# A fused attention and look-up FFN kernel: the look-up steps get places of their own on ScalarE and VectorE, and ScalarE makes all eight leaves

## The chip, the cores and the metric

The kernel runs on one core of a Trainium2 chip. The metric is the device time of one execution in microseconds, the median of several runs. The kernel before takes 1107.08 us (three runs, 1107.05 to 1108.62).

A core has five engines, each with its own queue of instructions that it works off strictly in order: PE (TensorE, matrix products), ACT (ScalarE), DVE (VectorE), POOL (GpSimd) and SP (SyncE, which here issues DMAs). They wait for each other by semaphores only.

## The reference, cut to what matters

x is 2 x 2048 x 512, the four attention matrices are 512 x 512. The three FFN matrices aren't given as numbers but as indices from 0 to 15 into a table `lut` of 16 values.

```python
def attn(x, Wq, Wk, Wv, Wo):            # x is layernormed
    q, k, v = x @ Wq, x @ Wk, x @ Wv    # einsum bse,ef->bsf
    scores = einsum('bes,bfs->bef', q^T, k^T) / sqrt(16)   # 512 x 512 per batch
    return einsum('bef,bfs->bes', softmax(scores), v^T)^T @ Wo

def ffn(x, lut, gate_idx, up_idx, down_idx):   # x is layernormed
    gate, up = x @ lut[gate_idx].T, x @ lut[up_idx].T      # 1376 x 512
    return (silu(gate) * up) @ lut[down_idx].T             # 512 x 1376

x = x + attn(layernorm(x), Wq, Wk, Wv, Wo)
x = x + ffn(layernorm(x), lut, gate_idx, up_idx, down_idx)
```

## The kernel before, in words

**Stages.** The 4096 tokens are 8 blocks of 512. First comes the Gram matrix of the normalised x for both batches (stage "gram", 32 steps). From it and the weights come, all as 512 x 512 products in four items each: PROD, SCORE (with its softmax), TURN_V, MIX and FOLD, for batch 0 and 1; in the end one matrix per batch stands for the whole attention. Then each block is multiplied by it ("attend"), added, normalised again, turned ("x2") and sent through the FFN: 11 chunks of 128 inner rows, for each a gate and an up product (24 matmuls of 128 x 512) and a down product (12). The first two blocks are interleaved by hand: in `first_plan` G is a gate and up product of the first block, H of the second, D a down product of the first, T, A and X prepare the second block. From the third block on the code is regular.

**Precision.** Every operand is split in a high part (ACT writes it with a cast: `mat_y_hi`, `x2t_hi`, `h_hi`, `w_hi`) and a low part (DVE subtracts: `mat_y_lo`, `x2t_lo`, `h_lo`, `w_lo`), and each product is three matmuls. So each result of PE goes over ACT and then over DVE before PE can use it again.

**The look-up.** The FFN weights, 33 tiles of 128 x 512 (tile u is gate, up or down of chunk u // 3), are built in SBUF from the indices beside all this. Per tile u: DVE takes the high bit of the index (`find_high`, L1249) and three masks of the lower bits (`find_bit`, L1244). For each of 8 values j of the three lower bits a *leaf* is made, lut[j] + high bit * (lut[j + 8] - lut[j]). Seven of them are ACT's (`make_leaves`, L791, one ACTIVATE each), leaf 4 is DVE's own (L1275, one TENSOR_SCALAR). Seven *merges* (`merge`, L1237, COPY_PREDICATED under a mask) then pick among the leaves into `picked`, ACT casts that to `w_hi` (`weight_high`, L808) and DVE subtracts for `w_lo` (`weight_low`, L1253). There is little room: the leaves share five `part` buffers and two `picked`, so a leaf waits until a merge has read what its buffer held, and merges wait for leaves. PE's gate product of chunk c waits for `w_lo` of tile 3c, the up product for that of 3c + 1, the down product for that of 3c + 2.

**The order.** One list, `timeline`, sets the order on all engines: each engine runs over it and does its own part of each entry. In the kernel before the look-up is in that list too. A tile is ten steps (`OPS`), and an entry ("look", k) makes ACT do the leaves that `leaves_at(k)` lists and DVE the k-th step of its generator `look_up`. So both engines have their look-up work at the same places of the list. How many steps go where is by constants for the first stages (`LOOKS_GRAM`, `LOOKS_TAKE`, `looks`), and for `first_plan` by `share`, which spreads what is left evenly over the time that PE is expected to need.

## Time and profile before

| what | us |
|---|---|
| median of three runs | 1107.08 |
| the profiled execution | 1108.86 |
| its span in the trace | 1107.0 |
| PE busy in the span | 1028.1 |
| DVE busy / ACT busy | 491.6 / 467.8 |

The page gives the busy time of each engine and cuts the span in slices. "Granted clock" (PEclk) is the share of its full 2.4 GHz that PE was given; at its lower level, 1.2 GHz, it is 0.5, and slices that hold both levels lie between. The look-up is all in the first 430 us. From there to the end PE is busy without gaps worth mentioning but for one of some 10 us before the last product; what happens there isn't touched by the change. In a row of a timeline an [x <-engine tile line] at the end is the idle time before that instruction and what ended it. Durations of neighbours overlap (an instruction starts before the one ahead has wholly ended), so that the pace of an engine is read from start to start.

### The profile page before, as it was taken

To read this page: it belongs to the slowest core of one execution; us is meant where nothing else is said; L and a number is where in the kernel's file an instruction comes from. 1 tells how busy PE (TensorE), PEld (TensorE's weight loads), DVE (VectorE), ACT (ScalarE), POOL (GpSimd) and SP (SyncE) were. 2 spreads that over 40 slices of the span, in tenths; PEclk is the share of its full clock that TensorE was granted. 3 is DMA by queue.
4 is the path that set the end of the run, shared out by engine and by line. 5 is a ranking of instruction groups with operands and counts; after the bars stand their busy time and mean duration, and the time that the engine had idled before them with its cause. 6 is when DMAs were issued, how large, how long until landed. Compare 5 with 4: busy or idle time off the path is not lost.

```text
span 1107.0 us, 13011 instructions
## 1 busy us (share of the span) xinstructions
PE 1028.1 (93%) x4744; PEld 844.5 (76%) x4744; DVE 491.6 (44%) x1016; ACT 467.8 (42%) x753; POOL 137.8 (12%) x135
## 2 busy tenths in 40 slices
PE   5888986979889897999999999999999999999997
PEld 4777775767668775788888888888888888888885
DVE  5786867978878987332213122312221222212001
ACT  4987767777867884122122212211221222122110
POOL 4422000000000000002011111111111111111111
PEclk9988998989979999999999999999999999999999
DMA  8853010230101114530022000201020010000000
GB/s 280 266 198 91 8 60 6 84 119 6 46 8 65 60 51 158 207 129 1 1 76 77 1 1 1 78 1 62 15 76 1 1 41 36 1 1 38 1 1 38
DMA packets 31756, 66.04 MB, mean 60 GB/s; under 512 B 3584, under 2 KB 17168, under 8 KB 27088
## 3 DMA queue, kind: packets, MB, share of 16 engines
q1 hardware_dynamic: 26912, 63.06, 15.9%
q10 hardware_dynamic: 4752, 2.16, 0.7%
q8 instruction: 39, 0.64, 0.2%
q0 software_dynamic: 32, 0.01, 0.1%
q14 instruction: 21, 0.17, 0.0%
HBM read 44.18 MB, written 21.04 MB: 59 GB/s over the span
## 4 chain that ended last, share of the span: by engine, by line
PE 66%; DVE 12%; ACT 12%; issue 8%; POOL 1%; DMA 1%; ACTq 0%; POOLq 0%; DVEq 0%
PE bank L1050 34%; PE bank L1058 19%; PE bank L992 8%; ACT part L791 4%; DVE part L1237 3%; PE bank L1093 2%; DVE picked L1237 2%; ACT picked L791 1%; PE bank L1006 1%; PE bank L1039 1%; DVE bn L1214 1%; DVE w_lo L1253 1%; ACT idx_out L872 1%; DVE part L1275 1%; ACT xg_n L882 1%
## 5 line engine op out<-in xcount | busy, mean ns | idle before, releaser
L1050 PE MATMUL bank<-x2t_hi,w_hi 128*128 128x512 f32 (+1 forms) x704 | 278.3, 395 | 22.6 <-ACT h_gate L944 10.3
L1050 PE MATMUL bank<-x2t_hi,w_lo 128*128 128x512 f32 (+1 forms) x704 | 276.8, 393 | 0.0
L1050 PE MATMUL bank<-x2t_lo,w_hi 128*128 128x512 f32 (+1 forms) x704 | 276.6, 393 | 0.0
L1450 DVE TENSOR_TENSOR h_full<-bank,h_gate 128x512 f32<-128x512 f32 (+1 forms) x66 | 45.6, 691 | 396.6 <-PE bank L1050 396.6
L1050 PEld LDWEIGHTS bank<-x2t_hi,w_hi 128*128 128x128 f32 (+1 forms) x704 | 132.1, 188 | 55.6 <-issue 20.6
L791 ACT ACTIVATE part<-high_bit,lut,lut_step 128x512 f32<-128x512 uint8 x198 | 155.4, 809 | 27.3 <-DVE part L1237 24.9
L1050 PEld LDWEIGHTS bank<-x2t_lo,w_hi 128*128 128x128 f32 (+1 forms) x704 | 132.1, 188 | 30.3
L1050 PEld LDWEIGHTS bank<-x2t_hi,w_lo 128*128 128x128 f32 (+1 forms) x704 | 132.4, 188 | 29.5
L740 POOL TENSOR_TENSOR h_lo<-h_full,h_hi 128x512 fp32r<-128x512 f32 (+1 forms) x66 | 85.2, 1291 | 508.1 <-ACT h_hi L968 508.1
L965 ACT ACTIVATE h_gate<-bank 128x512 f32<-128x512 f32 (+1 forms) x66 | 39.4, 598 | 256.3 <-PE bank L1050 256.3
L1058 PE MATMUL bank<-w_hi,h_hi 128*128 128x512 f32 (+1 forms) x324 | 129.6, 400 | 0.1
L1058 PE MATMUL bank<-w_lo,h_hi 128*128 128x512 f32 (+1 forms) x324 | 126.6, 391 | 0.0
L1058 PE MATMUL bank<-w_hi,h_lo 128*128 128x512 f32 (+1 forms) x324 | 126.3, 390 | 0.0
L968 ACT CAST h_hi<-h_full 128x512 fp32r<-128x512 f32 (+1 forms) x66 | 41.0, 621 | 188.2 <-DVE h_full L1450 188.2
L1237 DVE COPY_PREDICATED part<-bit_mask,part 128x512 f32<-128x512 uint8 x132 | 98.2, 744 | 1.2 <-ACT part L791 1.2
L745 POOL TENSOR_TENSOR rstd<-var,power 128x4 f32<-128x4 f32 x20 | 20.9, 1047 | 429.8 <-DVE var L1227 429.8
L1237 DVE COPY_PREDICATED picked<-bit_mask,part 128x512 f32<-128x512 uint8 x99 | 70.3, 739 | 1.6 <-ACT picked L791 1.6
L1058 PEld LDWEIGHTS bank<-w_lo,h_hi 128*128 128x128 f32 (+1 forms) x324 | 60.8, 188 | 13.1
L1058 PEld LDWEIGHTS bank<-w_hi,h_hi 128*128 128x128 f32 (+1 forms) x324 | 60.9, 188 | 12.1 <-POOL h_lo L740 0.5
L1058 PEld LDWEIGHTS bank<-w_hi,h_lo 128*128 128x128 f32 (+1 forms) x324 | 61.0, 188 | 11.7
L1093 PE MATMUL bank<-xg_hi 128*128 128x256 f32 (+2 forms) x128 | 46.9, 367 | 19.6 <-DVE xg_lo L1253 16.7
L992 PE MATMUL bank<-m_hi,xt_hi 128*128 128x512 f32 x112 | 44.1, 393 | 1.0 <-DVE xt_lo L1313 1.0
(148 smaller groups left out, 1353.3 us busy)
## 6 DMA issues: line engine op xcount, KB each, us to landing
xg<-in_L_attn_x SPq DMA_DIRECT2D x8, 1024.0 KB, 6.3
out_dram<-x1a SPq DMA_DIRECT2D x5, 1024.0 KB, 3.9
x1a<-in_L_attn_x SPq DMA_DIRECT2D x4, 1024.0 KB, 4.8
x1b<-in_L_attn_x SPq DMA_DIRECT2D x3, 1024.0 KB, 4.8
m_hi<-m_scratch SPq DMA_DIRECT2D x3, 1024.0 KB, 5.1
m_lo<-m_scratch SPq DMA_DIRECT2D x3, 1024.0 KB, 7.2
out_dram<-x1b SPq DMA_DIRECT2D x3, 1024.0 KB, 3.9
idx_raw<-in_L_ffn_gate_idx SPq DMA_DIRECT2D x10, 256.0 KB, 6.2
```

The lines of the kernel that those rows point to most:

```text
L740: return pool.tensor_tensor(out_, whole, high.bitcast(F32), ALU.subtract)
L745: pool.tensor_tensor(scale[:], var[:], power[:], ALU.pow).then_inc(rstd_made, 1)
L791: act.activation(tile, high, ACT.Identity, bias=entry, scale=step).then_inc(leaf_made, 1)
L872: act.copy(dst, src).then_inc(idx_laid, 1)
L965: act.activation(h_gate[0:n, :], bank[4][0:n, :], ACT.Silu).then_inc(silu_done, 1)
L968: act.copy(h_hi[c % 2][0:n, :], h_full[0:n, :]).then_inc(h_hi_done, 1)
L992: last = pe.matmul(out_, a, b, start=(i == 0 and j == 0), stop=(i == len(terms) - 1 and j == 2))
L1050: last = pe.matmul(tile[0:n, :], a, x, start=(k == 0 and j == 0), stop=(k == K - 1 and j == 2))
L1058: last = pe.matmul(bank[t][:], a, x, start=start and j == 0, stop=stop and j == 2)
L1093: last = pe.matmul(bank[4 * batch + m][:, cols], a[:, rows_of], b[:, cols], start=start and j == 0, stop=stop and j == 2)
L1237: return dve.copy_predicated(keep[:], bit_mask[bit][:], other[:])
L1450: dve.tensor_tensor(h_full[0:n, :], bank[5][0:n, :], h_gate[0:n, :], ALU.mult).then_inc(h_done, 1)
```

## The change

The constants and the function `share` that placed ("look", k) entries are gone, and with them these entries. Two strings take their place, `ACT_LOOKS` and `DVE_LOOKS`: the k-th character says, in base 36, how many look-up steps that engine does ahead of the k-th entry of the list. ACT gets a generator `look_up` of its own, with one step for each leaf, each fetch of indices and each `w_hi`. DVE's generator yields after nearly every instruction, so that its steps are smaller. Leaf 4, DVE's until now, goes to ACT: 33 instructions leave DVE, 33 come to ACT, and the semaphore `own_leaf_made` goes. Six of the eight leaves of tile u + 1 are made ahead of `w_hi` of tile u (`LEAVES_AHEAD`); before it was five of ACT's seven. PE, POOL and SP keep their instructions in their order.

```diff
-        LEAVES = [1, 0, 3, 2, 5, 6, 7]
-        OWN_LEAF = 4
-        LEAVES_NEXT = {4: [1], 5: [0], 6: [3], 7: [2], 8: [5]}
-        LEAVES_SAME = {1: [6], 2: [7]}
+        LEAVES = [1, 0, 3, 2, 5, 4, 6, 7]
+        LEAVES_AHEAD = 6
...
+        ACT_LOOKS = (
+            "0000000000000000000000000000000000000000000000000000000000000000000000000000000000000001000000000000"
...
+        def with_looks(counts, steps):
+            for k, entry in enumerate(timeline):
+                for _ in range(int(counts[k], 36) if k < len(counts) else 0):
+                    next(steps)
+                yield entry
+            assert next(steps, None) is None
...
+            def look_up():
+
+                yield from make_leaves(0, LEAVES[:LEAVES_AHEAD])
+                for u in range(U):
+                    yield from make_leaves(u, LEAVES[LEAVES_AHEAD:])
+                    if u + 1 < U:
+                        yield from make_leaves(u + 1, LEAVES[:LEAVES_AHEAD])
+                    act.wait_ge(picked_done, u + 1)
+                    if u + 3 < U:
+                        fetch_idx(u + 3)
+                        yield
+                    weight_high(u)
+                    yield
...
-            for stage, arg in timeline:
+            for stage, arg in with_looks(ACT_LOOKS, look_up()):
...
                     merge(0, y, z).then_inc(merged, 1)
-                    tile, high, step, entry = make_leaf(dve, u, OWN_LEAF)
-                    dve.tensor_scalar(tile, high, step, entry, ALU.mult, ALU.add).then_inc(own_leaf_made, 1)
                     yield
...
-                    dve.wait_ge(leaf_made, leaf_count(u, 5))
-                    dve.wait_ge(own_leaf_made, u + 1)
+                    dve.wait_ge(leaf_made, leaf_count(u, 4))
                     merge(0, w, five).then_inc(merged, 1)
```

**First place, ACT between the softmax and the FOLD stage.** `mat_y_hi` is the high part of a MIX product; a row with `lut_step` is a leaf, `w_hi` the cast of a finished tile. Before:

```order
L912 CAST wb_hi<-bank 128x4x128 x2
L791 ACTIVATE part_164<-high_bit_166,lut,lut_step 128x512
L912 CAST mat_y_hi_111<-bank 128x512
L835 ACTIVATE xn_first<-x1a,shift_kept_188,rstd_kept_186 128x512
L791 ACTIVATE part_162<-high_bit_166,lut,lut_step 128x512
L912 CAST mat_y_hi_111<-bank 128x512
L835 ACTIVATE xn_first<-x1a,shift_kept_188,rstd_kept_186 128x512
L791 ACTIVATE part_160<-high_bit_165,lut,lut_step 128x512
L791 ACTIVATE picked_158<-high_bit_165,lut,lut_step 128x512
L912 CAST mat_y_hi_111<-bank 128x512
L835 ACTIVATE xn_first<-x1a,shift_kept_188,rstd_kept_186 128x512
L791 ACTIVATE part_162<-high_bit_165,lut,lut_step 128x512
```

And now, from the last `wb_hi` on:

```order
L879 CAST wb_hi<-bank 128x4x128 x4
L879 CAST mat_y_hi_111<-bank 128x512
L802 ACTIVATE xn_first<-x1a,shift_kept_188,rstd_kept_186 128x512
L879 CAST mat_y_hi_111<-bank 128x512
L802 ACTIVATE xn_first<-x1a,shift_kept_188,rstd_kept_186 128x512
L879 CAST mat_y_hi_111<-bank 128x512
L802 ACTIVATE xn_first<-x1a,shift_kept_188,rstd_kept_186 128x512
```

Between the last `sbias` of the softmax and the last of the four `mat_y_hi`, ACT had 11 leaves and a `w_hi`; now it has 2 leaves. Nine leaves have moved ahead of it, among the softmax items, or behind it.

**Second place, ACT at the second block's x2.** From the silu of G4 (`h_gate`) to `x2t_hi`, the turned input of the second block. Before:

```order
L944 ACTIVATE h_gate<-bank 128x512
L791 ACTIVATE picked_159<-high_bit_166,lut,lut_step 128x512
L791 ACTIVATE part_162<-high_bit_166,lut,lut_step 128x512
L791 ACTIVATE part_161<-high_bit_166,lut,lut_step 128x512
L791 ACTIVATE part_160<-high_bit_166,lut,lut_step 128x512
L958 CAST h_hi_77<-h_full 128x512
L855 CAST x2t_hi<-bank 128x512 x2
L784 DMA idx_in_170<-idx_scratch 128x512
L808 CAST w_hi_55<-picked_158 128x512
L791 ACTIVATE part_164<-high_bit_166,lut,lut_step 128x512
L791 ACTIVATE part_162<-high_bit_166,lut,lut_step 128x512
L855 CAST x2t_hi<-bank 128x512 x2
```

And now:

```order
L907 ACTIVATE h_gate<-bank 128x512
L746 ACTIVATE part_160<-high_bit_166,lut,lut_step 128x512
L746 ACTIVATE part_163<-high_bit_166,lut,lut_step 128x512
L739 DMA idx_in_171<-idx_scratch 128x512
L761 CAST w_hi_54<-picked_158 128x512
L746 ACTIVATE part_164<-high_bit_166,lut,lut_step 128x512
L921 CAST h_hi_77<-h_full 128x512
L822 CAST x2t_hi<-bank 128x512 x2
L746 ACTIVATE part_162<-high_bit_166,lut,lut_step 128x512
L746 ACTIVATE part_160<-high_bit_165,lut,lut_step 128x512
L746 ACTIVATE picked_158<-high_bit_165,lut,lut_step 128x512
L822 CAST x2t_hi<-bank 128x512 x2
```

Here the count alone doesn't change (six leaves and a `w_hi`), but ahead of this piece, from the second block's normalisation `xn_second` on, it does: up to the silu of G4 there were 10 leaves and two `w_hi`, now there are 4 leaves and none.

**Third place, DVE in the steady part of `first_plan`.** A pair (G or H) gives `h_full`, ACT casts its high part, DVE subtracts for the low one. Before:

```order
L1244 TENSOR_SCALAR bit_mask_167<-idx_in_170 128x256
L1436 TENSOR_TENSOR h_full<-bank,h_gate 128x512
L1253 TENSOR_TENSOR h_kept_lo<-h_full,h_kept_hi 128x512
L1237 COPY_PREDICATED picked_159<-bit_mask_169,part_163 128x512
L1237 COPY_PREDICATED picked_158<-bit_mask_167,part_160 128x512
L1237 COPY_PREDICATED part_161<-bit_mask_167,part_162 128x512
L1275 TENSOR_SCALAR part_163<-high_bit_165,lut_step,lut 128x512
```

And now:

```order
L1200 COPY_PREDICATED part_163<-bit_mask_167,part_164 128x512
L1397 TENSOR_TENSOR h_full<-bank,h_gate 128x512
L1216 TENSOR_TENSOR w_lo_67<-picked_159,w_hi_56 128x512
L1216 TENSOR_TENSOR h_kept_lo<-h_full,h_kept_hi 128x512
L1200 COPY_PREDICATED part_160<-bit_mask_167,part_162 128x512
```

A look-up instruction now stands between `h_full` and the low part that waits for ACT's cast of it. Of the 14 pairs after the second block's x2 that still had look-up work behind them none had that before; now all 15 have at least one.

## Rows read from the trace of the kernel before

**Rows 1.** The page: the span, and PE's busy time, share and instructions.

```profile
span 1107.0 us, 13011 instructions
PE 1028.1 (93%) x4744; PEld 844.5 (76%) x4744; DVE 491.6 (44%) x1016; ACT 467.8 (42%) x753; POOL 137.8 (12%) x135
```

**Rows 2.** Stretches: length, busy per engine (instructions), PEclk, DMA share, GB/s.

```profile
0.00:153.97 153.97, 127.16 (x729) 110.66 (x729) 110.22 (x242) 115.45 (x200) 38.10 (x55) 0.96 0.50 162
153.97:181.40 27.43, 14.91 (x65) 11.75 (x64) 22.69 (x47) 23.90 (x45) 0.00 (x0) 0.86 0.02 5
181.40:239.95 58.55, 51.34 (x224) 41.16 (x225) 46.70 (x97) 41.49 (x64) 1.39 (x1) 0.94 0.20 76
239.95:311.44 71.49, 58.85 (x249) 47.34 (x249) 57.74 (x123) 53.69 (x81) 1.01 (x1) 0.88 0.10 39
311.44:425.90 114.46, 103.74 (x432) 83.44 (x432) 96.74 (x199) 89.27 (x133) 0.00 (x0) 0.96 0.13 46
425.90:1107.00 681.10, 672.13 (x3048) 550.17 (x3048) 157.51 (x313) 144.06 (x234) 97.26 (x78) 1.00 0.11 42
```

**Rows 3.** PE's timeline: start, us, instruction, idle before and its releaser.

```profile
159.56 0.50 PE L992 MATMUL bank<-wa_hi,mat_x_hi 128*128 128x512 f32 x1 [2.54 <-DVE mat_x_lo L1407]
...
181.40 0.76 PE L992 MATMUL bank<-mat_y_hi,wb_hi 128*128 128x512 f32 x1 [9.06 <-DVE mat_y_lo L1389]
...
239.95 0.77 PE L1050 MATMUL bank<-x2t_hi,w_hi 128*128 128x512 f32 x1 [6.16 <-DVE x2t_lo L1326]
...
291.71 0.47 PE L1050 MATMUL bank<-x2t_hi,w_hi 128*128 128x512 f32 x1 [1.98 <-ACT h_gate L944]
...
305.88 1.97 PE L1039 MATMUL bank<-ident,xn_second 128*128 128x128 f32 x8 [4.86 <-DVE x2t_lo L1326]
311.44 0.77 PE L1050 MATMUL bank<-x2t_hi,w_hi 128*128 128x512 f32 x1 [3.59 <-DVE x2t_lo L1326]
...
425.90 0.48 PE L1050 MATMUL bank<-x2t_hi,w_hi 128*96 128x512 f32 x1 [1.75 <-DVE w_lo L1253]
```

**Rows 4.** DVE's timeline in the softmax: one of three alike.

```profile
148.14 0.69 DVE L1253 TENSOR_TENSOR wa_lo<-raw,wa_hi 128x512 fp32r<-128x512 f32 x1 [0.38 <-ACT wa_hi L896]
```

**Rows 5.** ACT's timeline at the end of MIX.

```profile
178.58 1.52 ACT L791 ACTIVATE part<-high_bit,lut,lut_step 128x512 f32<-128x512 uint8 x2
179.99 0.58 ACT L912 CAST mat_y_hi<-bank 128x512 fp32r<-128x512 f32 x1
```

**Rows 6.** ACT's timeline at the first block's x2.

```profile
232.33 0.80 ACT L791 ACTIVATE part<-high_bit,lut,lut_step 128x512 f32<-128x512 uint8 x1
...
238.51 2.03 ACT L855 CAST x2t_hi<-bank 128x512 fp32r<-128x512 f32 x4
```

**Rows 7.** ACT's timeline at the second block's x2.

```profile
300.60 0.57 ACT L944 ACTIVATE h_gate<-bank 128x512 f32<-128x512 f32 x1
...
304.40 1.06 ACT L855 CAST x2t_hi<-bank 128x512 fp32r<-128x512 f32 x2
```

**Rows 8.** DVE's timeline around a pair in the steady part.

```profile
404.45 0.74 DVE L1237 COPY_PREDICATED part<-bit_mask,part 128x512 f32<-128x512 uint8 x1
405.10 0.53 DVE L1275 TENSOR_SCALAR part<-high_bit,lut_step,lut 128x512 f32<-128x512 uint8 x1
405.55 0.67 DVE L1436 TENSOR_TENSOR h_full<-bank,h_gate 128x512 f32<-128x512 f32 x1
406.91 0.69 DVE L1253 TENSOR_TENSOR h_kept_lo<-h_full,h_kept_hi 128x512 fp32r<-128x512 f32 x1 [0.69 <-ACT h_kept_hi L958]
```

**Rows 9.** Groups by line, 312 to 426 us: count, busy, mean ns, idle before.

```profile
L1253 DVE TENSOR_TENSOR h_kept_lo<-h_full,h_kept_hi 128x512 fp32r<-128x512 f32 x9 | 6.2, 692 | 8.0 <-ACT h_kept_hi L958 8.0
L1253 DVE TENSOR_TENSOR h_lo<-h_full,h_hi 128x512 fp32r<-128x512 f32 x5 | 3.5, 692 | 4.3 <-ACT h_hi L958 4.3
...
L791 ACT ACTIVATE part<-high_bit,lut,lut_step 128x512 f32<-128x512 uint8 x78 | 60.5, 807 | 8.8 <-DVE part L1237 8.7
L808 ACT CAST w_hi<-picked 128x512 fp32r<-128x512 f32 x13 | 8.0, 617 | 7.6 <-DVE picked L1237 6.7 <-issue 0.8
```

More of the change, by code:

```diff
@@ L305, in preln_attention_ghost_ffn @@
         timeline = []
-        looked = [0]
-        def look(n, limit):
-            for _ in range(min(n, OPS * limit - looked[0])):
-                timeline.append(("look", looked[0]))
-                looked[0] += 1
-                if looked[0] % OPS == 0:
-                    timeline.append(("built", looked[0] // OPS - 1))
         def settle(g):
@@ L323, in stats, with normalised @@
             timeline.append(("stats_shift", g))
-        def normalised(n, limit):
-            timeline.append(("norm", n))
-            look(1 if n < K * (number[(SCORE, 0)] + 1) else 2, limit)
-            timeline.append(("norm_low", n))
-        def room(n):
-            return 12 if n < K * (number[(MIX, 0)] + 1) else 15 if n < K * (number[(FOLD, 0)] + 1) else 21
+        def normalised(n):
+            timeline.extend([("norm", n), ("norm_low", n)])
         idx_per_tile = [(0, 1, 2, 2)[i % 4] if i < T * GB else (i >= T * GB + 4) + (i == T * NG - 1) for i in range(T * NG)]
@@ L1355, in _ @@
             first = one_block[0]
-            looks = look_up()
-            for stage, arg in timeline:
+            for stage, arg in with_looks(DVE_LOOKS, look_up()):
                 if stage == "lut_step":
```

104 lines of the change are left out of this document (36 added, 68 removed).

## The prediction, written before the changed kernel ran

> **What bounds the kernel now.** I read the page first. PE is busy for 1028.1 of 1107.0 us [rows 1], so the other engines matter only where PE waits for them. The stretches show where that is [rows 2]: behind 425.90 PE idles 9 us in 681, in front of it 70 us in 426 (153.97 - 127.16 = 26.8, then 12.5, 7.2, 12.6 and 10.7), with a granted clock under 1. Nothing behind 425.90 is touched, so whatever the change is worth is the time at which PE gets there.
>
> Then PE's own timeline for the gaps and what ended them [rows 3]. None of the large ones between 150 and 312 us is ended by the look-up itself. They end with `mat_x_lo`, `mat_y_lo`, `x2t_lo` or `h_gate`, results of ordinary products on their way over ACT and DVE. The reader is to see in ACT's rows why these were late: a row with `lut` stands right in front of the awaited cast [rows 5, 6]. The look-up is in the way there, not wanted there. Only in the last stretch it is the limit itself: the up product of chunk 10 waits for `w_lo` at 425.90 [rows 3]. There DVE is busy 96.7 of 114.5 us and ACT 89.3 [rows 2], and of DVE's idle 17.7 us, 12.3 go into 14 waits for ACT's cast of h [rows 9].
>
> **The change part by part.** The sum is made against the profiled execution: span 1107.0, time 1108.9, which is 1.8 over the median of 1107.08.
>
> *Softmax to MIX.* In the first batch's softmax a leaf stands between ACT's scaling and its cast `wa_hi`, and DVE idles 0.38 for it, three times [rows 4]; the new order puts the leaves behind the cast. The chain is later than PE already (PE waits 2.54 for it at 159.56 [rows 3]), so about 1 us comes back. Two leaves per item instead of one fit in DVE's and ACT's waits for each other. Bounds: 2.5 won (the gap gone), 2 lost (two leaves more than the waits hold, at 0.7 each, with a w_hi). I take -1.
>
> *MIX to FOLD, the largest gap.* PE stopped at 181.40 - 9.06 = 172.34. All it needs is one cast and one subtraction: 0.58 for `mat_y_hi` [rows 5], 0.69 as for DVE's other subtractions of this shape [rows 4], and some 0.2 between the engines: 1.5 us. In truth two leaves stand in front of the last cast [rows 5], and DVE had merges between too. The new order has no leaf among the four casts. 9.06 - 1.5 = 7.5 us won. Bounds: 7.5, and 4 if `xn_first`, which stays between, and late work from the softmax hold it up. I take -7.5.
>
> *First block's x2.* Its normalised rows are done when the leaf at 232.33 starts, and `x2t_hi` starts at 238.51: 6.2 us [rows 6]. Between them stood six leaves and two casts; now two leaves and the same two casts. From start to start a leaf takes 1.41 / 2 = 0.70 us [rows 5]. Four leaves less are 2.8 us, and one wait for a merge between them goes (0.7): -3.5 of the 6.16 [rows 3]. Bounds 2.5 and 4.7.
>
> *Second block's x2.* Three PE gaps belong together: 1.98, 4.86 and 3.59, sum 10.4 [rows 3]. ACT had 10 leaves and two w_hi between the normalisation and the silu of G4, now 4 leaves: 6 x 0.70 + 2 x 0.5 = 5.2 us earlier. The silu at 300.60 and `x2t_hi` at 304.40 [rows 7] come that much earlier, which covers the 4.86 and leaves about 2.4 of the three gaps. -8. Bounds 5 and 9.5.
>
> *The last stretch.* 311.44 to 425.90, 114.5 us. What was left out above has to be done here: of the merges, 106 instead of 96 remain behind the second x2, of the leaves 118 instead of 91. DVE: its 96.7 us of work [rows 2] grow by 10 merges at 0.65 (405.10 - 404.45 [rows 8]), masks and one pair (3.0), and shrink by 13 leaves of its own at 0.45 (405.55 - 405.10 [rows 8]): 96.7 + 6.5 + 3.0 - 5.9 = 100.3. The 0.69 behind each `h_full` [rows 8], 12.3 in all [rows 9], is filled by the look-up step that now stands there. ACT: 27 leaves more at 0.70, two w_hi and a pair more: 89.3 + 19 + 2.5 = 110.8 to the last tile, about 103 to tile 31, the one that the up product at 425.90 needs. PE's own work is 103.7, or 99 at the full clock. So three engines need 97 to 104 us where now 114.5 pass. Nothing says that the waits of ACT for merges vanish (8.7 and 6.7 [rows 9]); I leave 5 us for waits: 108, which is -6.5. Bounds: -11 with none, and the rivals below on the other side.
>
> The Trainium skill speaks against this part: "ScalarE: Activation LUTs", section "Rules for kernel authors", says that additions and multiplications belong on VectorE, not on ScalarE. The trace agrees on the price of one: the same leaf takes 0.45 us on DVE and 0.70 on ACT, by starts. By the rule the 33 leaves moved would cost 33 x 0.25 = 8 us of engine time; the rival "paid back with interest" below is what that would look like.
>
> *The clock.* PE got 0.86, 0.94, 0.88 and 0.96 in the four stretches behind 153.97 [rows 2]: 3.8 + 3.5 + 8.6 + 4.6 = 20 us of full-speed work not granted, part of it in the gaps. After the 9.06, 6.16 and 3.59 us gaps PE's first matmul lasts 0.76 to 0.77, after the 1.98 and 1.75 ones 0.47 to 0.48 [rows 3]: with short gaps the 2.4 GHz level stays. Between 0 and 9 us come back; I take -3.
>
> *The gram stage and new waits.* In 0 to 153.97 ACT is busiest of the three (115.4 with 110.2 for DVE [rows 2]); leaf work starts with smaller bites there and catches up by 70 us: -1 (bounds +2 and -3). Against all this +4 for waits that show only when the order changes, since ACT gets 33 x 0.70 = 23 us more work by 430 us. Bounds 0 and 10.
>
> Sum: -1 - 7.5 - 3.5 - 8 - 6.5 - 3 - 1 + 4 = -26.5. From the median: 1107.1 - 26.5 = 1080.6; I say **1081**.
>
> **The rivals.**
>
> *Paid back at the old pace.* The merges not yet done at the second x2 are 10 more, 1.4 tiles. Before, 96 merges (13.7 tiles) took 114.5 us there: 8.36 us a tile. If that pace is not one of busy engines but of the ring (leaf waits for merge, merge for leaf, w_hi for picked, five buffers), it stays: 106 / 7 = 15.1 tiles x 8.36 = 126.5, +12 in the last stretch. The stages ahead still bring -1 - 7.5 - 3.5 - 8 - 1 = -21. Sum -9: **1098**. For it: ACT waits for merges and `picked` for 15 us there [rows 9]. Against it: 12.3 of DVE's 17.7 idle us are at `h_lo` [rows 9] and not at merges, so that DVE's work and those waits set the pace.
>
> *Paid back with interest: slower.* One mechanism: ACT becomes the bound of the last stretch. Each tile takes the old pace and the eighth leaf on top, 8.36 + 0.70 = 9.06 us; 15.1 x 9.06 = 137, +22.5. The stages ahead bring -21, the clock nothing, and the waits of +4 stand: +5.5, **1112**. It is slower than before once a tile takes more than (114.5 + 17) / 15.1 = 8.7 us. For it: ACT's 110.8 us of work is more than PE's. Against it: ACT had 25 us idle there (114.5 - 89.3), and the 12.3 us that DVE waited at `h_lo` are filled whatever ACT does.
>
> *All waits gone.* The last stretch at 104, the clock with its 7 us, no new waits: 1107 - 1 - 7.5 - 4.5 - 9.5 - 10.5 - 7 = **1067**.
>
> *Nothing.* Another chain, hidden now, is just behind each gap and the gaps only change names: within 0.2%, 1107.
>
> **How the numbers follow.** My case 63% (1068 to 1092), old pace 19% (1092 to 1105), with interest 8%, all waits gone 7%, nothing 3%. 0.2%, or 2.2 us, is about what a measurement of this kernel tells from no change. Faster by more: 63 + 19 + 7 = 89%; within: 3%; slower: 8%. The range for 8 in 10 leaves out the outer parts of the last stretch's cases: **1068 to 1102**.
>
> **What the changed profile would show.** MIX to FOLD: a PE gap near 1.5 us, the clock still up behind it. x2t_lo of the first block: 2.7 us instead of 6.2. Second block: the three gaps together under 3. DVE in the last stretch: hardly any idle at `h_lo`, no line with own leaves, busy over 92%. ACT over 95% busy there, with leaves of 0.70 from start to start. PE's gaps there still end with `w_lo` or `h_gate`, some 5 to 8 us in sum. PE's part behind the look-up's end stays at its 681 us. I am wrong if the second x2 isn't some 20 us earlier than 311.44, or if the stretch from there to the up product of chunk 10 takes over 115 us.

## The result, and the profile after

The changed kernel takes **1059.28 us** (median of 4 runs, 1057.82 to 1060.47). The kernel before takes 1107.85 in the same series (4 runs). The ratio is 0.9561 with a 95% interval of 0.9544 to 0.9577. The forecast was 1081, range 1068 to 1102: the sign is right, and the gain is 48.6 us where 26 were forecast. The profiled execution has a span of 1058.6 us. In a few of the series below one or two executions took far longer than the others of their kernel; ratios and medians here leave them out.

The page of the changed kernel, span and PE, answers to [rows 1]:

```profile
span 1058.6 us, 12978 instructions
PE 1011.9 (96%) x4744; PEld 834.3 (79%) x4744; DVE 479.8 (45%) x983; ACT 486.9 (46%) x786; POOL 138.5 (13%) x135
```

PE has the same 4744 instructions and is busy 16.2 us less: the granted clock of the run rose from 0.973 to 0.992. Its idle time fell by 32.2, from 78.9 to 46.7.

To see where, both kernels are cut at the same work, not at the same time. The cuts are the first product behind the gram stage, the start of MIX, of FOLD, of the first gate, of the gate that waits for the second block's x2, and the up product of chunk 10. First the kernel before, where the cuts are not those of [rows 2] (columns as there):

```profile
0.00:108.06 108.06, 81.97 (x526) 73.77 (x527) 74.33 (x170) 81.28 (x138) 38.10 (x55) 0.94 0.66 211
108.06:159.56 51.50, 47.33 (x221) 38.54 (x219) 40.23 (x81) 38.42 (x72) 0.00 (x0) 1.00 0.13 42
159.56:181.40 21.84, 12.78 (x48) 10.09 (x49) 18.34 (x39) 19.65 (x35) 0.00 (x0) 0.83 0.01 3
```

Then the changed kernel, all seven stretches:

```profile
0.00:97.77 97.77, 75.87 (x527) 68.71 (x528) 74.54 (x169) 82.73 (x142) 38.78 (x55) 1.00 0.73 233
97.77:145.42 47.65, 46.61 (x220) 38.72 (x218) 43.02 (x90) 45.25 (x82) 0.00 (x0) 1.00 0.13 46
145.42:159.72 14.30, 11.76 (x48) 8.80 (x49) 11.79 (x23) 13.73 (x27) 0.00 (x0) 1.00 0.02 5
159.72:210.17 50.45, 49.09 (x224) 40.47 (x225) 44.47 (x91) 44.29 (x69) 1.40 (x1) 0.97 0.17 62
210.17:265.12 54.95, 52.94 (x248) 43.79 (x249) 48.10 (x99) 49.91 (x76) 1.05 (x1) 1.00 0.18 71
265.12:376.94 111.82, 103.55 (x432) 83.62 (x433) 101.66 (x205) 107.52 (x163) 0.00 (x0) 0.95 0.16 55
376.94:1058.60 681.66, 672.14 (x3048) 550.21 (x3048) 156.21 (x311) 143.48 (x233) 97.26 (x78) 1.00 0.11 41
```

Subtracting, with PE's idle as length less busy:

| stretch | before | after | difference | PE busy | PE idle | forecast, without the clock's -3 and +4 for waits |
|---|---|---|---|---|---|---|
| gram stage, to the first product | 108.06 | 97.77 | -10.3 | -6.1 | -4.2 | -1 |
| products and softmax, to MIX | 51.50 | 47.65 | -3.9 | -0.7 | -3.1 | -1 |
| MIX to FOLD | 21.84 | 14.30 | -7.5 | -1.0 | -6.5 | -7.5 |
| FOLD to the first gate | 58.55 | 50.45 | -8.1 | -2.3 | -5.9 | -3.5 |
| first gate to the second x2 | 71.49 | 54.95 | -16.5 | -5.9 | -10.6 | -8 |
| the last stretch | 114.46 | 111.82 | -2.6 | -0.2 | -2.5 | -6.5 |
| behind the look-up | 681.10 | 681.66 | +0.6 | 0 | +0.5 | 0 |

Each profile is one execution, and where its clock falls is in part chance. From FOLD to the first gate, e4, e6, e8, e9 and h2 below have the lists of the changed kernel and take 48.82 to 48.87 us at a clock of 1.00, where its own profile has 50.45 at 0.97. Differences of 1.6 us in a stretch are within that.

PE's gaps that answer to [rows 3] (start, us, instruction, idle before and its releaser), and the one new large gap, at 331.69:

```profile
145.42 0.50 PE L955 MATMUL bank<-wa_hi,mat_x_hi 128*128 128x512 f32 x1 [1.05 <-DVE mat_x_lo L1370]
159.72 0.47 PE L955 MATMUL bank<-mat_y_hi,wb_hi 128*128 128x512 f32 x1 [2.18 <-DVE mat_y_lo L1352]
210.17 0.47 PE L1013 MATMUL bank<-x2t_hi,w_hi 128*128 128x512 f32 x1 [1.36 <-DVE x2t_lo L1290]
265.12 0.47 PE L1013 MATMUL bank<-x2t_hi,w_hi 128*128 128x512 f32 x1 [2.02 <-DVE x2t_lo L1290]
331.69 0.79 PE L1013 MATMUL bank<-x2t_hi,w_hi 128*128 128x512 f32 x1 [3.59 <-DVE w_lo L1216]
376.94 0.47 PE L1013 MATMUL bank<-x2t_hi,w_hi 128*96 128x512 f32 x1 [3.43 <-DVE w_lo L1216]
```

The gaps of 9.06 and 6.16 us are now 2.18 and 1.36. The three of the second block (1.98, 4.86, 3.59) are one of 2.02, and one more of the kernel before, in the same stretch, is gone:

```profile
262.34 0.58 PE L992 MATMUL bank<-m_hi,xt_second_hi 128*128 128x512 f32 x1 [2.21 <-DVE xt_second_lo L1313]
```

Behind the first four gaps of the changed kernel PE starts with a product of 0.47 to 0.50 us; in the kernel before it took 0.76 or 0.77 behind 9.06, 6.16 and 3.59. But a short first product doesn't say that the clock stays up. Behind FOLD's gap it falls 0.5 us later, and the products are 0.43 us apart instead of 0.23:

```profile
160.30 0.63 PE L955 MATMUL bank<-mat_y_lo,wb_hi 128*128 128x512 f32 x1
160.73 0.63 PE L955 MATMUL bank<-mat_y_hi,wb_hi 128*128 128x512 f32 x1
```

ACT at the end of MIX, for [rows 5]: the casts now alternate with the normalisation alone, and the leaves follow.

```profile
154.73 0.61 ACT L879 CAST mat_y_hi<-bank 128x512 fp32r<-128x512 f32 x1
155.20 0.85 ACT L802 ACTIVATE xn_first<-x1a,shift_kept,rstd_kept 128x512 f32<-128x512 f32 x1
155.92 0.60 ACT L879 CAST mat_y_hi<-bank 128x512 fp32r<-128x512 f32 x1
...
158.29 0.61 ACT L879 CAST mat_y_hi<-bank 128x512 fp32r<-128x512 f32 x1
158.75 0.86 ACT L802 ACTIVATE xn_first<-x1a,shift_kept,rstd_kept 128x512 f32<-128x512 f32 x1
159.47 0.84 ACT L746 ACTIVATE picked<-high_bit,lut,lut_step 128x512 f32<-128x512 uint8 x1
```

DVE around a pair, for [rows 8]: two merges stand behind `h_full`, and the low part starts without a wait.

```profile
370.10 0.75 DVE L1200 COPY_PREDICATED part<-bit_mask,part 128x512 f32<-128x512 uint8 x1 [1.04 <-ACT part L746]
370.79 0.69 DVE L1397 TENSOR_TENSOR h_full<-bank,h_gate 128x512 f32<-128x512 f32 x1
371.39 0.74 DVE L1200 COPY_PREDICATED picked<-bit_mask,part 128x512 f32<-128x512 uint8 x1
372.03 0.73 DVE L1200 COPY_PREDICATED part<-bit_mask,part 128x512 f32<-128x512 uint8 x1
372.73 0.69 DVE L1216 TENSOR_TENSOR h_kept_lo<-h_full,h_kept_hi 128x512 fp32r<-128x512 f32 x1
```

The groups of the last stretch, 265 to 377, for [rows 9] (count, busy, mean ns, idle before). First ACT, then DVE:

```profile
L746 ACT ACTIVATE part<-high_bit,lut,lut_step 128x512 f32<-128x512 uint8 x103 | 77.9, 806 | 0.2 <-DVE picked L1200 0.2
L761 ACT CAST w_hi<-picked 128x512 fp32r<-128x512 f32 x15 | 9.1, 607 | 0.0
```

```profile
L1200 DVE COPY_PREDICATED part<-bit_mask,part 128x512 f32<-128x512 uint8 x58 | 43.1, 744 | 7.9 <-ACT part L746 7.9
L1216 DVE TENSOR_TENSOR h_kept_lo<-h_full,h_kept_hi 128x512 fp32r<-128x512 f32 x10 | 6.9, 690 | 0.2
```

ACT's waits for merges (8.7) and for `picked` (6.7) are gone and so are DVE's 12.3 us at the low parts. In their place DVE waits 7.9 us for leaves.

### The profile page after: what moved, and what is told of

Same layout as the page of the kernel before. It is cut to its first block, busy times and chain, and to the rows that moved or that the text cites. A ratio compares the mean times of both kernels' runs of the same rounds, so it can differ in the third digit from the quotient of the medians.

```text
span 1058.6 us, 12978 instructions
## 1 busy us (share of the span) xinstructions
PE 1011.9 (96%) x4744; PEld 834.3 (79%) x4744; DVE 479.8 (45%) x983; ACT 486.9 (46%) x786; POOL 138.5 (13%) x135
## 3 DMA queue, kind: packets, MB, share of 16 engines
q1 hardware_dynamic: 26912, 63.06, 16.5%
## 4 chain that ended last, share of the span: by engine, by line
PE 79%; DVE 9%; ACT 5%; issue 4%; DMA 1%; POOL 1%; ACTq 0%; POOLq 0%; SPq 0%; DVEq 0%
PE bank L1013 44%; PE bank L1021 22%; PE bank L955 9%; PE bank L1056 2%; DVE part L1200 2%; ACT part L746 1%; DVE picked L1200 1%; PE bank L969 1%; PE bank L1002 1%; DVE bn L1177 1%; ACT xg_n L849 1%; ACT idx_out L839 1%; DVE mat_x_lo L1370 1%; DMA idx_scratch<-idx_out 1%; DMA xg<-in_L_attn_x 0%
## 5 line engine op out<-in xcount | busy, mean ns | idle before, releaser
L1013 PE MATMUL bank<-x2t_hi,w_hi 128*128 128x512 f32 (+1 forms) x704 | 276.6, 393 | 12.3 <-DVE w_lo L1216 8.3
L746 ACT ACTIVATE part<-high_bit,lut,lut_step 128x512 f32<-128x512 uint8 x231 | 176.2, 810 | 3.7 <-DVE picked L1200 1.9
L1021 PEld LDWEIGHTS bank<-w_hi,h_lo 128*128 128x128 f32 (+1 forms) x324 | 61.1, 189 | 11.8
L1056 PE MATMUL bank<-xg_hi 128*128 128x256 f32 (+2 forms) x128 | 44.5, 348 | 18.6 <-DVE xg_lo L1216 16.1
```

The lines of the kernel that those rows point to most:

```text
L746: act.activation(tile, high, ACT.Identity, bias=entry, scale=step).then_inc(leaf_made, 1)
L1013: last = pe.matmul(tile[0:n, :], a, x, start=(k == 0 and j == 0), stop=(k == K - 1 and j == 2))
L1021: last = pe.matmul(bank[t][:], a, x, start=start and j == 0, stop=stop and j == 2)
L1056: last = pe.matmul(bank[4 * batch + m][:, cols], a[:, rows_of], b[:, cols], start=start and j == 0, stop=stop and j == 2)
```

## The experiments

In all tables of places, one number says how many look-up steps an engine takes before an entry of the program. The medians below stand beside the ratio to the kernel before of the same series. Times inside a kernel are from its profile.

### Places or leaf: e1_leaf_only, e2_places_only

e1 has the changed kernel's code, with the places computed from the kernel before. e2 keeps the new places and gives the leaf back to VectorE:

```
 e2:
+                    if j == 4 and u >= OWN_FROM:      # OWN_FROM = 0; ScalarE skips it
+                        yield
+                        continue
 ...
+                        dve.tensor_scalar(tile, high, step, entry, ALU.mult, ALU.add).then_inc(own_leaf_made, 1)
```

> One part alone: the places are those of the kernel before (each engine's look-up steps at the same entries of the list as there), but leaf 4 is ScalarE's, made just ahead of the cast w_hi of the tile in front. Theory 'places' (the gain of 48 us is all in where the look-up steps stand, since the gaps that went are those in front of mat_y_lo, x2t_lo and xg_lo): no gain, ACT gets 23 us more work at the same places, 1107 to 1116. Theory 'leaf' (what pays is that DVE is rid of 33 leaves of 0.45 us): the DVE-bound last stretch gets 6 us shorter, 1095 to 1102.

> The other part alone: the changed kernel's places, leaf 4 back on VectorE behind the second merge. Theory 'places': nearly all of the gain stays, 1056 to 1066, and below 1059 if ACT (96% busy in the last stretch of the changed kernel) is the bound there. Theory 'leaf': half the gain goes, 1075 or more.

e1: 1112.3 us, ratio 1.0043 (1.0028 to 1.0058). e2: 1063.33 us, 0.9595 (0.9572 to 0.9618). So the places bring 44 of the 48 us. The eighth leaf on ScalarE costs 4.6 in the old places. In the new ones the kernel with it is 4 us the faster, by intervals that still overlap (0.9544 to 0.9577 with it).

### Which half of the program: e3_gram_new, e4_gram_old

Tables spliced at the first product. e3 has the new places ahead of it and the old behind, e4 the reverse; eight leaves on ScalarE in both. Steps that one list has left over at the seam stand right behind it.

> The changed kernel's places up to the first product (about 100 us), from there on those of the kernel before, with leaf 4 on ScalarE throughout. If the gains of the stages add up, the 10.3 us of the gram stage stay against e1_leaf_only: e1 minus 10. If a stage behind it gives them back, because the look-up's end sets the time and the look-up isn't further on, e1 minus 0 to 3.

> The reverse: the places of the kernel before up to the first product, the changed kernel's behind it. If the gains add up: 1059 + 10 = 1069. If they don't: 1059 to 1062.

e3: 1099.71 (0.9936, 0.9912 to 0.9961), 12.6 less than e1. e4: 1071.09 (0.9667, 0.9646 to 0.9689), 11.8 more than the changed kernel. Both ways the gram stage's places are worth about 12 us at the end, and the two halves add. Nothing won there is paid back later, and this is the term that the forecast had at 1.

### Is it the clock: f1_fill_fold, f2_fill_gram

Both are the kernel before, with products in PE's gaps that nobody reads: f1 in front of FOLD (34, shown) and of the first gate (20, not shown), f2 in three gaps of the gram stage, where a wait also moves ahead of them.

```
 f1:
+                    if n == K * number[(FOLD, 0)]:
+                        for _ in range(34):
+                            pe.matmul(product_bank(n)[:], wa[0][:, 0, 0:P], wa[0][:, 0, :], start=True, stop=True)
 f2, one of three places:
+                    pe.wait_ge(xg_lo_done, i + 1)
                     if i == T * GB:
+                        for _ in range(16):
+                            pe.matmul(bank[3][:, 0:2 * P], xg_hi[i % 4][:, 0:P], xg_hi[i % 4][:, 0:2 * P], start=True, stop=True)
                         pe.wait_ge(idx_laid, U_HIGH_BANKS)
-                    pe.wait_ge(xg_lo_done, i + 1)
```

> The kernel before, with PE kept busy in its two longest gaps: 34 products of 128x512 in front of FOLD (gap 9.06 us at 181.40) and 20 in front of the first gate product (gap 6.16 us at 239.95), into banks that nobody reads. The look-up stays where it was, so the gaps' ends come from ACT and DVE as before. Theory 1, the clock is a loss of its own: PE then starts FOLD and the first gate at 2.4 GHz (first product 0.50 us instead of 0.76 and 0.77), each of the two pieces is 2 to 2.6 us shorter, and the end comes 3 to 5 us earlier: 1103 to 1105. Theory 2, PE's arrival is not what the next wait hangs on: the two pieces get shorter but the gaps at 291 to 311 us end when they did, and the time is 1107.7 within 1 us.

> The kernel before, with products of 256 columns in three PE gaps of the gram stage: 16 in the one of 2.74 us at 56.98, 18 in the one of 3.21 at 70.60, 12 in the one of 2.23 at 94.02, all into columns that nobody reads. Theory 1, the changed kernel is 10 us earlier at the first product because PE kept the high clock there: the granted clock between 45 and 100 us goes from 0.90 to 0.97 or more and the first product comes at least 4 us before 108.06; time 1104 or less. Theory 2, ACT sets the pace and its 9 us of waits (4.6 for shift, 2.5 for picked, 1.5 for PE) are what went: clock up as well, first product earlier by less than 2 us, time 1106 to 1108.

f1 at FOLD, PE's timeline; the row of the kernel before is the second of [rows 3]:

```profile
180.69 0.39 PE L1130 MATMUL bank<-wa_hi 128*128 128x512 f32 x1
181.13 0.50 PE L992 MATMUL bank<-mat_y_hi,wb_hi 128*128 128x512 f32 x1
181.47 0.39 PE L992 MATMUL bank<-mat_y_hi,wb_lo 128*128 128x512 f32 x1
```

FOLD starts when it did (181.13 for 181.40) but with products 0.23 apart instead of 0.43, and the next piece comes at 186.71 instead of 189.83, 3.1 us earlier. The lead reaches the first block's `x2t_lo`, which starts at 235.93 and not at 239.1. It doesn't reach PE, because the second filler holds PE until 240.07, 3.3 us longer than `x2t_lo` does:

```profile
233.92 6.31 PE L1147 MATMUL bank<-w_hi 128*128 128x512 f32 x20 [3.33 <-DVE mat_x_lo L1396]
240.07 0.39 PE L1050 MATMUL bank<-x2t_hi,w_hi 128*128 128x512 f32 x1
```

So the first filler's gain was spent by the second, and what is left is the piece behind the first gate, 2.6 us shorter. The profile has a lead of 3.6 us at the up product of chunk 10 and of 3.1 at its end. The median says less: 1105.9, ratio 0.9989 (0.9978 to 1.0001), under the 3 to 5 that theory 1 gave and not clear of no change. f2: 1105.85, 0.9989 (0.9979 to 1.0), between the theories. Its first product is 2.5 us earlier, but that of h4 below, which runs the same instructions up to there as the kernel before, is 2.4 earlier as well. In single profiles the lower level costs 2.6 to 3.1 us at such a place; in the medians each of the two kernels wins 1.2 us, and no run brings 10.

### Which engine's places count in the gram stage: g1_act_new, g3_shift_first, g4_look_later

g1 is the changed kernel with VectorE's table spliced as in e4 and ScalarE's left new. g3 and g4 change a line each of the kernel before:

```
 g3:
-            look(LOOKS_GRAM if i >= FIRST_LOOK else 0, 12)
             if 1 <= g < NG - 1 and t == T - 1:
                 timeline.append(("stats_shift", g + 1))
+            look(LOOKS_GRAM if i >= FIRST_LOOK else 0, 12)
 g4:
-    FIRST_LOOK = 8
+    FIRST_LOOK = 16
```

> The changed kernel, with VectorE's look-up steps up to the first product where they were before, and ScalarE's where they are now. With both in the old places up to there the kernel took 1071.1, with both new 1059.3. Theory 1, VectorE's merges in front of its shift made ScalarE late (4.6 us of waits for shift before, 0.5 after): most of the 11.8 us is lost again, 1067 to 1072. Theory 2, ScalarE's leaves in front of its own casts made the gram stage late: the new places on ScalarE alone bring most of it, 1059 to 1063.

> The kernel before, with the look-up step that stands in front of shift of groups 2 to 7 in the gram stage put behind it. Theory 1, merges in front of shift are what makes ScalarE wait 4.6 us for it and PE behind: the first product comes 2 us or more before 108.06, 1103 to 1105.5. Theory 2, VectorE is late as a whole there, and moving one step in ten changes nothing: 1106 to 1108.

> The kernel before, with the look-up beginning at gram step 16 instead of 8, so that eight steps fewer are done by the first product (some 5.6 us of ScalarE, 4 of VectorE) and come later. Theory 1, the gram stage is bound by the two engines' sums of work and the gain there is work put off to where PE does not wait: the first product comes 4 to 8 us earlier than 108.06; by the end some of it is paid in the last stretch (8 steps in 10 a tile at 8.36 us), net 1101 to 1106. Theory 2, the place of each step counts and not their number: first product earlier by under 2 us, and the end later by up to 6, 1107 to 1114.

g1: 1071.85 (0.9673, 0.9651 to 0.9695), as slow as e4. ACT's normalisation of the tokens between 45 and 100 us, in the kernel before and in g1:

```profile
L882 ACT ACTIVATE xg_n<-xg,shift,rstd 128x512 f32<-128x512 f32 x17 | 13.8, 811 | 4.6 <-DVE shift L1232 4.6
```

```profile
L849 ACT ACTIVATE xg_n<-xg,shift,rstd 128x512 f32<-128x512 f32 x17 | 14.0, 823 | 8.3 <-DVE shift L1195 8.3
```

In the changed kernel that wait is 0.5 us. VectorE's new places are needed for the gain. But g1 is no clean return to the old state. VectorE's merges in their old places now wait for leaves that ScalarE makes in its new ones, and they stand in front of `shift`. From 30 us to the first product, g1 (two lines) and the kernel before:

```profile
L1200 DVE COPY_PREDICATED part<-bit_mask,part 128x512 f32<-128x512 uint8 x10 | 8.5, 854 | 8.9 <-ACT part L746 8.9
L1200 DVE COPY_PREDICATED picked<-bit_mask,part 128x512 f32<-128x512 uint8 x7 | 5.5, 779 | 3.3 <-ACT picked L746 3.3
```

```profile
L1237 DVE COPY_PREDICATED picked<-bit_mask,part 128x512 f32<-128x512 uint8 x7 | 5.7, 814 | 1.6 <-ACT picked L791 1.6
```

The merges wait 12.2 us in g1 and 1.6 before. g1 shows that ScalarE's new places alone bring nothing here; it doesn't show that the merges alone made the statistics late in the kernel before. The reverse, VectorE's new places with ScalarE's old ones, was not run.

The clock is a small part of it. The first product comes at 108.06 with a granted clock of 0.94 over the stage (the kernel before), at 107.77 with 0.98 (e1), at 109.09 with 0.94 (e4), at 109.44 with 0.98 (g1) and at 105.56 with 0.98 (f2). The best of these is 2.5 us ahead of the kernel before; the changed kernel, with 1.00, is 10.3 ahead.

g3: 1107.13 (0.9992, 0.9983 to 1.0), first product 1.0 earlier, less than h4 is without any edit there. It is not the single step in front of `shift`. g4: first product 4.8 earlier, 8.2 at 276 us, 3.9 at 448; 1105.19 (0.9983, 0.9968 to 0.9997), at the upper end of theory 1. Putting work off does bring PE forward: g4 has made 18 leaves and 12 merges at its first product, the kernel before 25 and 17. But done crudely, half of it is paid back later. The changed kernel does something else. At its first product it has made 24 leaves and 19 merges, as much as before, 10 us earlier. Its lists have 9 and 5 steps fewer in front of that entry, but the old lists' are not all done either when PE gets there. What changed is where the steps stand, and not how many are done.

### MIX to FOLD alone: h1_mix_held

The kernel before, with the eight steps among MIX's four items behind the fourth:

```
-            look(1, room(n))
+            look(0 if group == (MIX, 0) else 1, room(n))
-            look(looks - 1, room(n))
+            look((0, 8)[m == K - 1] if group == (MIX, 0) else looks - 1, room(n))
```

> The kernel before, with one place changed: the eight look-up steps that stood among the four items of MIX of the first batch stand behind the fourth, so that no leaf is between the mat_y_hi casts. Theory 1, the stages' gains add and stay: FOLD starts 6 to 8 us before 181.40 with the clock up, and the end comes 6 to 8 us earlier, 1100 to 1102. Theory 2, the steps held back push the same work behind: FOLD starts as early, but the gap before the first gate product or those around 300 us grow by 3 us or more, and the time is 1104 to 1108.

1103.86 (0.9967, 0.9956 to 0.9979). FOLD starts 3.5 us earlier, and the profile ends 3.8 earlier. The time lies just between the two theories. The gain stays, as theory 1 says, but it is half the size: the gap is 5.66. Five leaves are gone from between the casts, while in front of the first `mat_y_hi` there are still those among the `wb_hi` casts and in the softmax, which the new places moved as well.

### The last stretch: h2_dve_behind, h4_before_fill

h2 is the changed kernel with the 29 steps between `h_full` and its low part put behind the low part (table entries moved by one). h4 is the opposite in the kernel before, three lines:

```
-                timeline += [("h_full", item), ("h_high", item), ("h_low", item)]
+                timeline += [("h_full", item), ("h_high", item)]
+                look(1, U)
+                timeline.append(("h_low", item))
```

> The changed kernel, with the look-up steps that VectorE has between h_full and the low part of it in the last stretch (29 steps, 14 pairs) behind the low part, as they stood before the change. VectorE then waits 0.69 us for each cast again, 10 us in 15 pairs. Theory 1, filling these waits is what the last stretch won: the up product of chunk 10 comes 3 to 8 us later, time 1062 to 1067. Theory 2, VectorE then loses at h_lo what it now loses at the leaves (7.9 us), since ScalarE is the busier one: 1059 to 1061.

> The kernel before, with one look-up step of those that stand behind the low part of h put in front of it, in each pair, so that VectorE has something to do while ScalarE casts; nothing else is moved and the leaves stay seven on ScalarE. Theory 1, these waits (12.3 us of VectorE's idle time in the last stretch) are time of the last stretch: it gets 6 to 12 us shorter, 1095 to 1101. Theory 2, h_lo is then later and with it the down products, or ScalarE's waits for merges take the time: 1104 or more.

h2: 1072.82 (0.9687, 0.9674 to 0.97), 13.5 us slower than the changed kernel, well over the 3 to 8 of theory 1. Its last stretch takes 122.66 us, 10.8 more. DVE's groups there:

```profile
L1216 DVE TENSOR_TENSOR h_kept_lo<-h_full,h_kept_hi 128x512 fp32r<-128x512 f32 x10 | 6.9, 693 | 9.7 <-ACT h_kept_hi L921 9.7
L1216 DVE TENSOR_TENSOR h_lo<-h_full,h_hi 128x512 fp32r<-128x512 f32 x5 | 3.5, 693 | 3.4 <-ACT h_hi L921 3.4
```

h4: 1096.25 (0.9894, 0.9874 to 0.9914), 11.7 faster than before by the ratio, with one step moved in each pair. Its last stretch (304.62 to 410.60) is 106.0 us for 114.5, and DVE's idle time at the low parts, 12.3 in [rows 9], is 4.5:

```profile
L1255 DVE TENSOR_TENSOR h_kept_lo<-h_full,h_kept_hi 128x512 fp32r<-128x512 f32 x9 | 6.2, 692 | 3.1 <-ACT h_kept_hi L960 2.8
L1255 DVE TENSOR_TENSOR h_lo<-h_full,h_hi 128x512 fp32r<-128x512 f32 x5 | 3.5, 692 | 1.4 <-ACT h_hi L960 1.2
```

Its profile is 15.3 us ahead at the up product of chunk 10. 3.8 of them were there before the first gate, where nothing was moved, and 3.0 came from there to the second x2, where the edit acts but the clock was also 0.92 for 0.88. The 8.5 of the last stretch are the edit's.

### What bounds the last stretch now: e6_own_from18, e8_own_some, e9_leaf_free, e10_merge_small, e12_both_less

e6 and e8 give leaf 4 back to VectorE from tile 18 on, in every tile or every second one (as in e2). e9 leaves it out there, e10 cuts a merge to 64 columns, and e12 does both:

```
 e10:
-                    merge(0, w, five).then_inc(merged, 1)
+                    n = 64 if u >= 18 else D
+                    dve.copy_predicated(w[:, 0:n], bit_mask[0][:, 0:n], five[:, 0:n]).then_inc(merged, 1)
```

> The changed kernel, with leaf 4 of tiles 18 to 32 (those of the last stretch) on VectorE again: ScalarE has 15 x 0.70 = 10.5 us less work there, VectorE 15 x 0.45 = 6.8 more. Theory 1, ScalarE (busy 107.5 of 111.8 us) is what bounds the last stretch: the up product of chunk 10 comes 2 to 5 us earlier than 376.94, time 1055 to 1057.5. Theory 2, what bounds it is the ring of leaf and merge, in which VectorE (101.7 us, idle 7.9 for leaves) is the other half: the leaf on VectorE stretches its half as much, 1059 to 1063.

> As before this one, but leaf 4 goes back to VectorE only in every second tile from 18 on (8 tiles): ScalarE 5.6 us less, to 102; VectorE 3.6 more, to 105. Theory 1, the sums of work bound the stretch: this is the best balance of the three and 3 to 5 us faster than 1059.3. Theory 2, the ring bounds it: within 1.5 us of 1059.3.

> The changed kernel without leaf 4 of tiles 18 to 32 on either engine: the merge takes what the tile held before, so this part of the look-up is left out. ScalarE has 10.5 us less work and VectorE the same. Theory 1, ScalarE is the bound of the last stretch: it shortens until PE (103.6 us busy, 99 at the full clock) or VectorE (101.7) is the bound, 6 to 9 us, time 1050 to 1053. Theory 2, it is not: under 2 us, 1057 to 1060.

> The changed kernel with one merge in six cut from 512 to 64 columns in tiles 18 to 32 (the one of leaves 4 and 5; the rest of its columns is left out of the look-up): VectorE has 15 x 0.5 = 8 us less work in the last stretch, ScalarE the same. Theory 1, VectorE's chain (101.7 us of work and 7.9 of waits in 111.8) bounds the stretch: the up product of chunk 10 comes 4 to 8 us earlier, time 1051 to 1056. Theory 2, each engine's share is bound by the other's order (taking a leaf from ScalarE brought 0): under 1.5 us, 1058 to 1061.

> The changed kernel with both reliefs in tiles 18 to 32: leaf 4 left out (ScalarE 10.5 us less) and the merge of it cut to 64 columns (VectorE 6 us less by the run with that alone). Theory 1, the two engines are loaded alike and each hides the other's relief: together the last stretch gets 4 to 8 us shorter than 111.8, 1052 to 1056. Theory 2, the order of the steps and PE's own 99 us set it: under 2.5 us, 1057 to 1059.

| kernel | time | ratio (interval) | last stretch | ACT busy | DVE busy |
|---|---|---|---|---|---|
| changed | 1059.28 | 0.9561 (0.9544 to 0.9577) | 111.8 | 107.5 | 101.7 |
| e6 | 1061.69 | 0.9582 (0.9568 to 0.9595) | 113.4 | 98.0 | 107.5 |
| e8 | 1061.31 | 0.9585 (0.9572 to 0.9599) | 112.9 | 102.6 | 104.6 |
| e9 | 1059.8 | 0.9569 (0.9556 to 0.9582) | 110.5 | 98.1 | 101.5 |
| e10 | 1058.46 | 0.9546 (0.9529 to 0.9563) | 110.0 | 106.9 | 95.4 |
| e12 | 1056.73 | 0.9530 (0.9518 to 0.9543) | 108.5 | 97.6 | 94.9 |

The last stretch of the changed kernel also runs, without any edit, in e4 and g1, and takes 110.7 there; so 110.0 and 110.5 are hardly shorter. e6 is where theory 2 has it, and e8 is 2 us slower than the changed kernel, which neither theory has (the intervals overlap). In e9 ScalarE has 10 us less to do and nothing is won: theory 1 of it is wrong. DVE still waits for leaves:

```profile
L1208 DVE COPY_PREDICATED part<-bit_mask,part 128x512 f32<-128x512 uint8 x59 | 43.8, 743 | 6.7 <-ACT part L754 6.6
```

DVE's relief alone brings 0.8 us by the medians and 1.7 by the ratios, with intervals that overlap: nothing that can be told from none. The same wait grows to 10.5 in e10:

```profile
L1200 DVE COPY_PREDICATED part<-bit_mask,part 128x512 f32<-128x512 uint8 x43 | 31.9, 742 | 10.5 <-ACT part L746 10.1
```

Both together bring 3.3 us of the stretch and 2.6 of the time, under the 4 that theory 1 asked for, and the wait is still 8.0. That leaves the order: a leaf stands behind a cast or a silu, and that waits for PE (ACT's idle time before `h_gate` is 2.9 us in the changed kernel and 6.0 in e9). This is argued from the waits and not shown; a better order was not tried.

At the up product of chunk 10, e9 is 1.6 us ahead of the changed kernel, and at 399 us nothing of it is left. The clock fell behind the last gap, of 3.41 us; in the changed kernel the product behind the gap of 3.43 is one of 0.47, and the clock stays up:

```profile
375.29 0.74 PE L1021 MATMUL bank<-x2t_hi,w_hi 128*96 128x512 f32 x1 [3.41 <-DVE w_lo L1224]
```

### A faster kernel: f3_fill_after

The changed kernel, with 7 unread products in front of FOLD and 12 in front of the up products of chunks 8 and 10:

```
-                        pe.wait_ge(w_lo_done, 3 * c + kind + 1)
                         if same_before(arg):
                             pe.wait_ge(read, same_before(arg))
+                        if b == 0 and kind == 1 and c in (8, 10):
+                            for _ in range(12):
+                                pe.matmul(pair_bank(arg)[1][:], w_hi[0][:, 0, 0:P], w_hi[0][:, 0, :], start=True, stop=True)
+                        pe.wait_ge(w_lo_done, 3 * c + kind + 1)
```

> The changed kernel with products of 128x512 that nobody reads in what is left of PE's gaps: 7 in front of FOLD (gap 2.18 us) and 12 in front of the up products of chunks 8 and 10 (3.59 and 3.43 us). Theory 1, the level that PE loses behind 331.69 (0.66 of the clock in that 10 us) is time of its own: the piece behind it is 1.5 to 2.5 us shorter and the end 1 to 2 us earlier, 1057 to 1058.5. Theory 2, the next wait for w_lo takes it back, since VectorE sets the pace there: within 0.7 us of 1059.3.

**1055.97 us** (5 runs, 1055.84 to 1057.08), ratio 0.9530 (0.9517 to 0.9543): 3.3 less than the changed kernel and the fastest of the complete kernels, more than theory 1 gave. All five runs are below all four of the changed kernel (1057.82 to 1060.47), and the intervals just don't meet. The granted clock is 0.996 or 0.997 in each of the five and 0.992 or 0.993 in each of the four.

Where the time is won, one profile doesn't tell. PE is 1.6 us earlier behind FOLD, 1.6 behind the second x2 and 1.0 behind the gap at 331.69. But FOLD to the first gate takes 48.87 us here and 48.82 to 48.87 in e4, e6, e8, e9 and h2, which have none, and in front of the piece behind the second x2 f3 has no filler either: g1, which has none at all, takes 58.43 us for it, f3 58.52 and the changed kernel 60.10.

## Why the forecast was wrong, step by step

The sum missed by 22 us. By the table, 9.3 of them are the gram stage, 8.5 the stretch to the second x2, 4.6 FOLD to the first gate and 2.9 the softmax; 3.9 went the other way in the last stretch. Cut otherwise, PE's idle time fell by 32.2 where the terms for waits add up to 23.5, and its busy time, which for the same instructions is the clock, by 16.2 where I had 3.

- **The gram stage: the step that failed.** -1 was forecast, -10.3 came, and 12 at the end by e3 and e4. I sized it by amounts: ACT's busy time, and leaf work that "starts with smaller bites there and catches up by 70 us". It does catch up (15 leaves and 10 merges at 70 us, before it was 14 and 8), so that by amounts there was nothing to win. I had not asked what each engine waits for there: ACT waited 4.6 us for `shift`, and now 0.5. PE's gaps of this stage were not in my list, and ACT isn't "busiest of the three" either: [rows 2] have PE at 127.2 and ACT at 115.4. e3 and e4 show that the steps' places in this stage are worth the 12 us; g1 shows that ScalarE's alone aren't enough, and with a clock of 0.98 in the old places the first product is only 0.3 (e1) to 2.5 us (f2) earlier. Which of the moved steps does it stays open.
- **Softmax to MIX: too small.** -1 was forecast (bounds to -2.5) and -3.9 came. I had expected to get back 1 us of PE's wait of 2.54 in front of MIX. It gave 1.5 (1.05 is left), and a gap of 0.92 at 156.36 is gone too. No run tests this stage by itself.
- **MIX to FOLD: right, the size with some luck.** -7.5 was forecast for the gap and -7.5 measured for the stretch. The gap gave 6.9 (2.18 are left instead of 1.5), the clock inside the stretch 1.0, and small waits took 0.4 back. The clock was up behind the gap for half a microsecond only. h1 shows that the steps among the casts are half of the gap.
- **First block's x2: right, a little too small.** The gap went from 6.16 to 1.36, -4.8, where I had -3.5 (bounds to 4.7). The other 3.3 us of that stretch are products at the full clock (2.3) and small waits.
- **Second block's x2: mechanism right.** My three gaps fell from 10.4 to 2.0, -8.4 where I had -8. What I had not counted is the gap of 2.21 at 262.34, which went too, and 5.9 us less of busy time. No run moves the steps of one of these two places alone; that the leaves held them up is read from ACT's rows and the gaps.
- **The clock: mis-sized.** I took -3 for all behind 153.97, bounds 0 to 9. PE is busy 9.4 us less behind the start of MIX and 16.2 in all. I had counted 20 us not granted and supposed that the waits would take most of it back. How much of the 16 is time of its own is open: f1 and f2 win 1.2 us each by their ratios, hardly clear of nothing, f3 3.3.
- **The last stretch: mis-sized.** Busy times came as worked out (DVE 101.7 for 100.3, ACT 107.5 for 110.8, PE 103.6). I had 108 and it took 111.8, or 110.7 in e4 and g1. What I left for waits, 5 us, was 10 on DVE, 7.9 of it for leaves. The idle time at the low parts is what paid for the stretch: without the filling it takes 122.7 us (h2), near the 126.5 of the rival "paid back at the old pace". So that rival was not far off in the pace, and the filled waits kept it away.
- **The slower rival: did not happen**, though ACT is at 96% in the last stretch. e1 is what it looks like with the old places, +4.6. The rule of the Trainium skill, "ScalarE: Activation LUTs", section "Rules for kernel authors", that such arithmetic belongs on VectorE agrees with e1 and not with e2 or e6. With the new places the leaf on ScalarE is no worse; the medians are 4 and 2.4 us in its favour, with intervals that overlap.
- **+4 for new waits: too much.** The gaps at 308.74 and 331.69, 4.5 us, are new, and stand in the last stretch's sum already.

## What to carry to other kernels

Look for an instruction that waits for another engine right behind its own input's producer, and put independent work in between. One moved step a pair was worth 11.7 us alone (h4), more than shifting whole leaves between the engines (+4.6 and -4). Size such a change by all stages where the helper's work stands, those with small gaps too, and read there what each helper engine waits for, not its busy share or the amount of work. When two engines feed each other, relieving one of them alone can bring nothing (e9), and moving the work of one alone can make new waits for the other (g1). Before a stage of one profile is compared with that of another, look how far it differs between kernels that are the same up to there.
